# Q products of two token blocks by seven half-size products in place of eight, and two output products of a step moved into the next one

## The reference

```python
    Q = (q @ Wq.T).reshape(b, s, HKV, exp, DK)      # q = _layernorm(x), exp = 4, DK = 128
    K = (k @ Wk.T).reshape(b, s, HKV, DK)           # k = v = ctx
    V = (v @ Wv.T).reshape(b, s, HKV, DV)
    scores = jnp.einsum('bqhed,bkhd->bheqk', Q, K) * scale      # causal mask, softmax
    attn = jnp.einsum('bheqk,bkhd->bqhed', probs, V)
    return attn.reshape(b, s, H * DV) @ Wd.T
...
x = x + jnp.tanh(g_xattn[0]) * _L0_xattn_ref(_layernorm(x, axis=-1), ctx, ctx, Wq, Wk, Wv, Wd)
x = x + jnp.tanh(g_ffn[0]) * _L0_ffn_ref(_layernorm(x, axis=-1), qweight, scale, zero_point, bias)
```

## Time and profile before

| | before |
|---|---|
| median of 3 runs (lowest, highest) | 1063.35 us (1062.31, 1066.21) |
| the profiled execution, device time | 1062.54 us |
| its span, first to last instruction | 1060.6 us |
| PE busy | 1019.3 us, 96% |
| DVE busy | 685.5 us, 65% |
| ACT busy | 456.7 us, 43% |
| POOL busy | 235.5 us, 22% |
| mean granted TensorE clock | 0.994 |

### The profile page before, as it was taken

The page is one execution under the profiler, slowest core; times in us unless marked ns, Lnnn a source line. Parts: engine busy times, 40 slices in busy tenths (PEclk is TensorE's granted clock), DMA queues, the critical chain, the costliest instruction groups (busy, mean ns, idle before and its releaser), DMA issues.

```text
span 1060.6 us, 19976 instructions
## 1 busy us (share of the span) xinstructions
PE 1019.3 (96%) x7842; PEld 569.6 (54%) x7842; DVE 685.5 (65%) x1374; ACT 456.7 (43%) x917; POOL 235.5 (22%) x245
## 2 busy tenths in 40 slices
PE   4889999999998999999999999999999999999995
PEld 2455555555554555555555555555555555555542
DVE  5856677777578665765466556665556664555678
ACT  5777676676532343233334332244433323333322
POOL 1355565565604000210001200210000400000013
PEclk9999999999999999999999999999999999999998
DMA  7648655445355432444313643234333443223111
GB/s 276 217 155 286 209 163 186 160 132 158 103 176 200 96 87 96 159 130 136 107 56 112 198 138 122 78 121 120 126 117 118 131 136 115 62 96 134 69 37 60
DMA packets 90219, 142.61 MB, mean 134 GB/s; under 512 B 31248, under 2 KB 64016, under 8 KB 79504
## 3 DMA queue, kind: packets, MB, share of 16 engines
q1 hardware_dynamic: 90128, 141.34, 41.5%
...
## 4 chain that ended last, share of the span: by engine, by line
PE 86%; DVE 10%; ACT 2%; issue 2%; DMA 1%; SPq 0%; DVEq 0%; ACTq 0%
PE pa L1295 42%; PE py L1295 29%; PE av L1408 5%; PE pp L1391 3%; PE ps L1375 2%; PE py L1466 2%; PE pp L1375 2%; DVE q L897 1%; DVE wq L897 1%; DVE sc L943 1%; DVE row_max L941 1%; DVE sc L937 1%; DVE sc L954 1%; DVE xn L1053 1%; DMA xacc<-in_x 1%
## 5 line engine op out<-in xcount | busy, mean ns | idle before, releaser
L1295 PE MATMUL pa<-xT,wq 128*128 128x512 f16 x1536 | 344.4, 380 | 10.2 <-DVE q L897 7.5
L1295 PE MATMUL py<-wd,att 128*128 128x512 f16 x1488 | 336.2, 379 | 0.7 <-issue 0.7
L1295 PEld LDWEIGHTS pa<-xT,wq 128*128 128x128 f16 x1536 | 146.1, 98 | 192.0 <-issue 25.9
L1295 PEld LDWEIGHTS py<-wd,att 128*128 128x128 f16 x1488 | 143.2, 98 | 159.2 <-issue 1.1
L677 ACT ACTIVATE q<-pa 128x512 f16<-128x512 f32 x128 | 75.7, 591 | 264.8 <-PE pa L1295 264.8
L976 DVE SCALAR_TENSOR_TENSOR xacc<-py,f_y,xacc 128x512 f32<-128x512 f32 x128 | 95.7, 748 | 124.2 <-PE py L1295 124.2
L728 ACT ACTIVATE att<-av 128x256 f16<-128x256 f32 x256 | 80.8, 384 | 145.8 <-PE av L1408 145.3
L967 DVE SCALAR_TENSOR_TENSOR att<-av,att 128x256 f16<-128x256 f32 x256 | 93.5, 418 | 67.1 <-ACT att L728 66.9
L897 DVE SCALAR_TENSOR_TENSOR q<-pa,q 128x512 f16<-128x512 f32 x128 | 87.9, 686 | 58.7 <-ACT q L677 55.9
L1295 PE MATMUL pa<-wv,cT 128*128 128x128 f16 x1536 | 96.2, 219 | 0.0
L1295 PEld LDWEIGHTS pa<-wv,cT 128*128 128x128 f16 x1536 | 89.8, 98 | 0.9
...
## 6 DMA issues: line engine op xcount, KB each, us to landing
wq<-kept_q SPq DMA_DIRECT2D x24, 1024.0 KB, 7.1
wd<-kept_d SPq DMA_DIRECT2D x23, 1024.0 KB, 4.8
v_dup<-v_nat SPq DMA_DIRECT2D x128, 128.0 KB, 2.4
raw_d<-in_wdT SPq DMA_DIRECT2D x8, 1024.0 KB, 10.2
kept_q<-wq SPq DMA_DIRECT2D x8, 1024.0 KB, 8.0
kept_d<-wd SPq DMA_DIRECT2D x8, 1024.0 KB, 5.2
raw_q<-in_wqT SPq DMA_DIRECT2D x7, 1024.0 KB, 5.4
...
```

Source lines behind the costliest of these rows:

```text
L1295: last = pe.matmul(out, stationary(a, i), moving(b, i), start=(i == 0 and (a, b) == PASSES[0]), stop=(i == count - 1 and (a, b) == PASSES[ ...
```

## The change

Q of steps `m` = 16 to 31 (the last two blocks) is computed by the seven-product scheme: heads are taken in two pairs `r`, each weight pair and the activations are cut into quadrants (head x half of the contraction, half of the contraction x half of the tokens), and `run(m, r, i)` is one half product: 2 chunks x 3 passes = 6 matmuls of 256 columns. Seven runs for each pair, 14 for a step, replace four heads. Runs 5, 6, 7 and 4 take mixed operands (sums and differences of quadrants): mixed weights `ws` and mixed activations `tT`. ACT copies three partial results of a pair out of PSUM (`copy_p1`, `copy_p5`, `copy_u2`), DVE adds later ones to them (`add_11`, `add_22`, `add_12`), and ACT and DVE take HI and LO parts of four quadrants (`hi_*`, `lo_*`). `Q_SCALE` and the scaling of the squares change by a power of two.

The mixed weights are made in steps 13 to 20 (`mixing(n)` is the group): SP loads a group's raw weights again (`load_mix`), POOL mixes them (`mix_weights`), ACT and DVE split them (`mix_hi`, `mix_lo`), and SP keeps them (`keep_mix`) and brings them back in block 3 (`back_mix`). The mixed activations of blocks 2 and 3 are made in steps 12 and 20 (`mix_norm`, `mixed_hi`, `mixed_lo`) and transposed by 32 further DMA transposes each; 8 of the 32 plain ones fall away. The norm that feeds the next block is a step earlier in blocks 1 and 2 (step 3 of the block in place of 4), and `ffn_weight` is done in steps 9 and 10 in place of 8 and 9.

From step 14 on `y_unit(n, 2)` and `y_unit(n, 3)` are issued among the Q runs of step `n + 1`, with their `y_part`, and `back_d` behind the first transposes of a step. Tiles were moved to other storage to make room.

```diff
-            return 6 if tb == 0 else 4
+            return 6 if tb == 0 else 3
...
+        FIRST_FAST = 2 * GROUPS
+        RUN = ((0, 1), (0, 5), (0, 2), (0, 6), (0, 7), (0, 3), (1, 1), (1, 5), (1, 2), (1, 6), (1, 7), (1, 3))
+
+        def fast(m):
+
+            return FIRST_FAST <= m < STEPS
...
+        def deferred(n):
+
+            return fast(n + 2)
...
+        BANK_X, BANK_Y, BANK_Z = (pa[0], av[1]), (pa[1], pa[1]), (av[0], av[0])
...
+            def transpose_first(n):
+
+                g, tb = n % GROUPS, n // GROUPS
+                if tb > 0 and g in (1, 2):
+                    call = NORMS.index((2, tb - 1))
+                    transpose_norm(call, transposes(call)[16 * (g - 1):16 * (g - 1) + 8])
+                if 0 < tb < BLOCKS - 1:
+                    call = NORMS.index((1, tb + 1))
+                    if g in (4, 5):
+                        transpose_norm(call, transposes(call)[16 * (g - 4):16 * (g - 4) + 8])
+                    elif g == 6:
+                        transpose_mixed(tb + 1, MIXED[12:20])
+
+            def transpose_rest(n):
+
+                g, tb = n % GROUPS, n // GROUPS
+                if tb > 0 and g in (1, 2):
+                    call = NORMS.index((2, tb - 1))
+                    transpose_norm(call, transposes(call)[16 * (g - 1) + 8:16 * g])
+                if 0 < tb < BLOCKS - 1:
+                    call = NORMS.index((1, tb + 1))
+                    if g == 4:
+                        transpose_norm(call, transposes(call)[8:16])
+                    elif g == 5:
+                        transpose_mixed(tb + 1, MIXED[0:12])
+                    elif g == 6:
+                        transpose_mixed(tb + 1, MIXED[20:32])
...
+                if m + 1 >= FIRST_FAST + GROUPS and fast(m + 1):
+                    back_mix(m + 1)
+                transpose_first(n)
+                if fast(m) and n < LAST:
+                    back_d(n)
+                transpose_rest(n)
                 if m < STEPS:
                     duplicate_v(m)
                 if ffn_of(n) is not None:
                     for t in range(ffn_of(n) * TILES, (ffn_of(n) + 1) * TILES):
                         store(t)
+                if mixing(n) is not None:
+                    keep_mix(mixing(n))
+                if mixing(n + 1) is not None:
+                    load_mix(mixing(n + 1))
...
+                pool.tensor_tensor(a22, a22, a21, ALU.add).then_inc(s_mix, 1)
+                pool.tensor_tensor(a21, a11, a21, ALU.subtract).then_inc(s_mix, 1)
+                pool.wait_ge(s_mix, 4 * g + 2)
+                pool.tensor_tensor(a11, a22, a11, ALU.subtract).then_inc(s_mix, 1)
+                pool.wait_ge(s_mix, 4 * g + 3)
+                pool.tensor_tensor(a12, a12, a11, ALU.subtract).then_inc(s_mix, 1)
...
+                if mixing(n) is not None:
+                    mix_weights(mixing(n))
+                if mix_of(n) is not None:
+                    mix_norm(mix_of(n))
+                    for t in range(TILES):
+                        mixed_lo(mix_of(n), t)
...
+                if fast(m):
+                    copy_p1(m, 0)
+                    exp(n, 0)
+                    copy_p5(m, 0)
+                    copy_u2(m, 0)
+                    exp(n, 1)
+                    hi_11(m, 0)
+                    p_part(n, 0)
+                    p_part(n, 1)
+                    hi_22(m, 0)
+                    hi_12(m, 0)
+                    copy_p1(m, 1)
+                    hi_21(m, 0)
+                    copy_p5(m, 1)
+                    copy_u2(m, 1)
+                    hi_11(m, 1)
+                    hi_22(m, 1)
+                    hi_12(m, 1)
+                    p_transposed(n, 0)
+                    hi_21(m, 1)
+                    if mixing(n) is not None:
+                        mix_hi(mixing(n), (0, 1))
...
+            def add_22(m, r):
+
+                dve.wait_ge(r_mm, run_count(m, r, 7))
+                dve.wait_ge(p5_ok, pair_count(m, r))
+                dve.tensor_tensor(p5, half(BANK_X[r]), p5, ALU.add).then_inc(c22_ok, 1)
...
+                if fast(m):
+                    scores(n, 0)
+                    scores(n, 1)
+                    add_11(m, 0)
+                    normalise(n, 0)
+                    normalise(n, 1)
+                    p_part(n, 0)
+                    add_22(m, 0)
+                    add_12(m, 0)
+                    y_late(2)
+                    lo_11(m, 0)
+                    lo_22(m, 0)
+                    lo_12(m, 0)
+                    lo_21(m, 0)
+                    p_part(n, 1)
+                    add_11(m, 1)
+                    y_late(3)
+                    add_22(m, 1)
+                    add_12(m, 1)
+                    lo_11(m, 1)
+                    lo_22(m, 1)
+                    lo_12(m, 1)
+                    lo_21(m, 1)
+                    if ffn is not None:
+                        ffn_scaled(t0)
+                    k_part(m)
+                    if mixing(n) is not None:
+                        mix_lo(mixing(n), (0, 1))
...
+                if (r, i) == (0, 1):
+                    pe.wait_ge(q_back[m % 2], backs(m))
+                    if m < FIRST_FAST + GROUPS:
+                        pe.wait_ge(s_hi, HPG * (m - FIRST_FAST + 1))
+                        pe.wait_ge(s_lo, HPG * (m - FIRST_FAST + 1))
+                    else:
+                        pe.wait_ge(s_back[m % 2], 16 * ((m - FIRST_FAST - GROUPS) // 2 + 1))
+                    if m % GROUPS == 0:
+                        transposed(pe, NORMS.index((1, tb)))
+                        pe.wait_ge(t_ld, 16 * len(MIXED) * (tb - 1))
+                    pe.wait_ge(k_hi, m)
+                    pe.wait_ge(k_lo, m)
+                elif (r, i) == (0, 5):
+                    pe.wait_ge(v_hi, m)
+                    pe.wait_ge(v_lo, m)
+                elif (r, i) == (0, 2):
+                    pe.wait_ge(av_hi, 4 * (m - 1) - 1)
+                    pe.wait_ge(av_lo, 4 * (m - 1) - 1)
+                elif (r, i) == (1, 1):
+                    pe.wait_ge(av_hi, 4 * (m - 1))
+                    pe.wait_ge(av_lo, 4 * (m - 1))
+                elif (r, i) == (1, 5):
+                    pe.wait_ge(c12_ok, pair_count(m, 0))
+                elif (r, i) == (1, 2):
+                    pe.wait_ge(c11_ok, pair_count(m, 0))
+                elif i == 6:
+                    pe.wait_ge(p1_ok, pair_count(m, r))
+                elif i == 7:
+                    pe.wait_ge(u2_ok, pair_count(m, r))
+                elif i == 3:
+                    pe.wait_ge(p5_ok, pair_count(m, r))
+                elif i == 4:
+                    pe.wait_ge(c22_ok, pair_count(m, r))
...
+                for kc in range(2):
+                    for c, d in PASSES:
+                        first = kc == 0 and (c, d) == PASSES[0]
+                        last = pe.matmul(half(bank), a[:, c, head, w_half + kc, :], b[:, d, b_half + kc, at],
+                                         start=first and i in (1, 2, 5),
+                                         stop=kc == 1 and (c, d) == PASSES[-1],
+                                         skip_group_check=i in (3, 4, 6, 7))
...
+                    run(m, 0, 1)
+                    run(m, 0, 5)
+                    run(m, 0, 2)
+                    run(m, 0, 6)
+                    y_unit(n - 1, 2)
+                    run(m, 0, 7)
+                    run(m, 0, 3)
+                    run(m, 1, 1)
+                    run(m, 0, 4)
+                    run(m, 1, 5)
+                    run(m, 1, 2)
+                    run(m, 1, 6)
+                    y_unit(n - 1, 3)
+                    run(m, 1, 7)
+                    run(m, 1, 3)
+                    p_transpose(n, 0)
+                    run(m, 1, 4)
+                    if ffn is not None:
+                        ffn_unit(t0, n)
+                    k_unit(m)
...
+                if deferred(n):
+                    continue```

On PE the order of a step changes as follows. Before, in step 16 (`pp<-k,q` and `ps<-k,q` are the scores, `pa<-xT,wq` is Q, `pa<-cT,wk` is K, `pa<-wv,cT` is V):

```order
L1375 MATMUL pp<-k,q 128x32 x24
L1375 MATMUL ps<-k,q 128x64 x24
L1295 MATMUL pa<-xT,wq 128x512 x48
L1391 MATMUL pp<-ident,pr 128x128 x8
L1295 MATMUL pa<-cT,wk 128x512 x12
```

More of the change, by code:

```diff
@@ L26 @@
 STEPS = BLOCKS * GROUPS
+HB = BT // 2
+HK = D // 2
 HI, LO = 0, 1
@@ L801, in _ @@
                     v_part(m)
+                if mixing(n) is not None:
+                    mix_hi(mixing(n), range(HPG))
                 if prep:
@@ L1204, in _ @@
                 for j in range(TILES):
-                    if n < LAST - 1:
+                    if n < LAST - 1 and not (deferred(n) and j >= 2):
                         y_part(n, j)
```

412 lines of the change are left out of this document (327 added, 85 removed).

## The result

| | before | after |
|---|---|---|
| median (lowest, highest) | 1063.18 us (1062.31, 1066.21) | 1095.61 us (1094.52, 1098.63) |
| span of the profiled execution | 1060.6 us | 1092.9 us |

The ratio is 1.030, 95% interval 1.027 to 1.033: slower by 32 us. The direction was forecast (slower, 1076.0); the size lies outside the range, which ended at 1087.

The account below looks back on a forecast made before the run. PE, busy 96% of the span, was taken as the bound. From 1062.54 us: -23.0 - 4.6 + 0.4 + 1.3 + 19.7 + 14.6 + 5.1 = +13.5, giving 1076.0 us; range 1054 to 1087.

Parts of the forecast that it names:

- The columns: Q by fourteen runs: 84 matmuls at 0.109 us, 9.14 in place of 10.58; -1.44 us a step, -23.0 over 16.
- Block 1: Step 9's `ffn_weight` stall goes, -4.6; meeting `ln_bn` and `ln_stats`, +0.4; `mix_hi` ahead of `av_part` 2 in step 13, +1.3.
- `add_22` in a plain step: `run(m, 0, 4)` waits for DVE's addition, S - 0.9 with DVE starting its chain at S = +1.6: 0.7 us, bounds 0.5 to 0.9.
- DVE's extra work at a step's end makes S larger: S, DVE's chain start, comes later in steps with norm or `ffn_zero` tails; all `add_22` stalls together +19.7 us.
- rival (d): Worse: short waits cost clock too (+5), and POOL's mixing slows DVE or SP's lateness reaches K or V: 1088; chance 0.08.
- SP's queue: Late transposes and loads: PE waits 7.2 us in step 15, 3.6 in step 23, 3.8 for wd in step 20; +14.6.
- SP is also behind by some 2 us: Step 14: SP's lag from steps 12 and 13, raising the transposes' lateness for step 15 from 6.1 to 8.2 us.
- the wait of step 23: PE waits for block 3's mixed transposes, landing at +34.4 against PE's 30.8: +3.6 us, plus 1.65 for the clock.
- Step 20: 3.5 us on `add_22` from `ln_norm` and four `ffn_zero` (S = 4.4), 3.8 waiting for wd, 1.65 for the clock.
- ACT's copies fit between: Q runs: ACT copies partial results in time, p1 by +2.6 for a run at +3.3, so no wait was added.
- The clock: Waits longer than 2.9 us, in steps 15, 20 and 23, cost 1.65 us each, +5.1; shorter ones nothing.
- The rule that I weighed and set aside: The throttled clock is the default, so no wait is safe; pricing waits of steps 18, 19 and 26 would add 5 us.

Follow-up runs that it names:

- e9: The changed kernel, seven products only in steps 26 to 30, mixing in steps 12-15 and 21, block 2's norm back, last `ffn_zero` spread: 1052.78 us, 0.991 of before.
- e3: The changed kernel with no mixed weights or activations made, kept or transposed; runs read plain tiles, output not the reference's: 1060.03 us, 0.998 of the kernel before.
- e2: The changed kernel without POOL's mixing of weights; loads, splits and transposes stay, output not the reference's: 1090.10 us, 1.027 of the kernel before.
- e7: The changed kernel with `duplicate_v`, `keep_mix` and `load_mix` issued by POOL in place of SP: 1113.58 us, 1.048 of the kernel before.
- e8: The kernel with plain operands and none mixed, with the next block's norm again at step 4 of blocks 1 and 2: 1056.36 us, 0.994 of the kernel before.

## Why the prediction was right in direction and wrong in size

**The columns: right.** 0.109 us a matmul, 9.14 for Q: the plain step shows a run of 0.65 and lasts 29.11, within 0.04 of 28.83 + 0.24 of waiting. The gain of 1.44 us a step was there, 23 over 16 steps.

**Block 1: right**, -4.06 in step 9 against -4.6 + 0.4, and +1.35 in step 13 against +1.3. Step 12 lost 0.75 that had no term: PE waits there for a DVE split of Q, in the step in which the mixed activations are made; e9 shows the same 0.75 in step 20, to which it moves this, and in e3, which makes none, step 12 loses 0.3.

**`add_22` in a plain step: right in kind, 0.24 in place of 0.7 us.** Start to start the two additions and `p_part` take 0.33 or 0.34 each, not 0.41. That is 0.24 of the 0.32 by which the chain is shorter, 7.00 in place of 7.32; the 0.07 for an overlap at its end wasn't there either. The lower bound that I named, 0.34, was the right value for the addition, but the 0.5 us that I worked out from it was not.

**"DVE's extra work at a step's end makes S larger": right where POOL is quiet, mis-sized beside it.** The terms for steps 16 to 19 were 1.6, 0.85, 2.0 and 2.4, 6.85 together. After lost 14.0 there (3.0, 3.3, 2.8, 4.9 over 28.83, or 35.88 in step 19). Without POOL's mixing, e2, it is 7.4. Of the 6.6 us between the two, 1.7 are the clock in step 19. The failing step is that I took DVE's durations from step 22, a step in which POOL was quiet, and put POOL into rival (d), with 0.08, though step 9 of the same trace shows the slower ones. Rows of both engines in one step show it: 128x256 from two SBUF tiles took 1.48 us in place of 0.42. The Trainium skill, "GPSIMD Engine Reference", section "Specifications", says that GpSimd's SBUF interfaces are shared with VectorE, with contention for DVE instructions that have two SBUF inputs. The trace agrees, down to the addition with a PSUM input, which stays at 0.41.

**SP's queue: the mechanism right, the lag too small.** 26.7 us for 20 transposes held to 0.1. "SP is also behind by some 2 us" was the failing step: the transposes began at +9.45, where the sum had 4.7 and that lag of 2 on top. `duplicate_v` of the step before stood ahead (3.1 us), and the four loads of weights took 4.0 us from first issue to the first transpose, 499.76 - 495.78, in place of 2.15. The lag came from step 13, whose 20 transposes began only at +6.5. My own sum gave 8.2 us late, and I took 7.2 without a reason; that is 1 us of the miss. The wait was 11.1 us against 7.2 forecast, and step 15 13.8 over 28.83 against 8.9. e7 fits the lag: with the transposes at +2.3 the wait is 6.4.

In step 22 I gave 0.7, and it lost 5.6, and here too it is the lag that failed. By my numbers `back_d(22)` would be issued at 4.0 + 2.2 + 8 x 1.33 = +16.9 and land 4.8 later, ahead of PE, which wanted it at +23.1; I didn't write that down, but it gives no wait. It was issued at +21.2. I had step 21's mixed transposes begin at +14.4, when the y unit is done. But SP came late out of step 20: the eight plain transposes of step 21, which begins at 733.99, were issued from +6.5 to +18.6, and only then came `back_d(21)` and the twelve mixed ones:

```profile
740.47 12.14 SPq L467 DMA_TRANSPOSE xT<-xh  x8
752.71 0.53 SPq L430 DMA_DIRECT2D wd<-kept_d  x1
```

For the wait of step 23 I forecast 5.3 us with the clock, and 4.5 were measured: that fits the same lag, less what PE had already lost in step 22.

**Step 20: right in sum, 10.75 against 9.0, not in its parts.** PE waited 2.0 us for a copy by ACT, 2.3 for `add_22`, and 3.1 for `pT`; wd was in time. The first two are one cause. DVE began the step's scores at +6.3 (700.68 - 694.41), not at S = 4.4: three `ffn_zero` took 4.0 us, not 3 x 0.66, with POOL's `ln_lo` of the moved norm beside them. On ACT two of the copies stand behind `exp(n, 0)`, and that waited for DVE:

```profile
696.75 4.01 DVE L1438 SCALAR_TENSOR_TENSOR xacc<-ff_rows,small,xacc 128x512 f32<-128x512 f32 x3
...
703.49 1.49 DVE L1277 TENSOR_TENSOR sc<-sc,row_max 128x512 f32<-128x512 f32 x1
```

```profile
695.92 5.85 POOL L657 TENSOR_TENSOR xh<-xn,xh 128x512 f16<-128x512 f32 x4 [26.13 <-ACT xh L875]
```

```profile
702.10 0.42 ACT L887 ACTIVATE sc<-sc 128x256 f32<-128x256 f32 x1 [4.50 <-DVE sc L1277]
```

So "ACT's copies fit between" failed here, and DVE's term was mis-sized by POOL once more. The wait for `pT` goes in e2, with the mixing; there the wait for wd appears, which in the changed kernel was hidden behind it.

**The clock: the price right for a short wait, the condition wrong.** I priced waits of at least 2.9 us at 1.65 each and shorter ones at nothing. (Three waits at 1.65 are 4.95; my sum has 5.1.) Step 15 paid more: behind its 11.1 us PE worked 5.2 us, 527.93 to 533.12, with the clock granted at 0.50, which is some 2.6 us lost. After step 19's wait of 2.81 and step 26's of 2.06 the clock fell too, after step 18's of 2.55 it did not. The windows of 3.3 us behind these waits (busy, granted clock), in this order step 18, 19 and 26:

```profile
633.21:636.50 3.29, 3.29 (x28) 1.00 0.27 47
665.20:668.50 3.30, 3.30 (x21) 0.66 0.01 2
904.07:907.37 3.30, 3.30 (x21) 0.67 0.07 15
```

The rule that I weighed and set aside, that no wait is safe as such, would have added 5 us; two of its three waits, 3.3 us, came true.

**The sum.** Against the forecast the span lost 18.8 us more: steps 16 to 19 +7.2, step 15 +4.9, step 22 +4.9, step 20 +1.75, steps 21, 25 and 26 +3.6, steps 9 to 13 +0.95; steps 23, 24 and 27 to 30 gave back 2.8, and what lies ahead of step 8 1.6. Some 9 of it is SP's queue (steps 15, 22 and 23) and what the clock cost behind it, 7 POOL beside DVE (steps 16 to 19, clock included), the rest clock and small tails. Rival (d), at 1088, named POOL beside DVE and the clock behind short waits, and both came. It also named lateness on SP, but for K or V, where it was wd and the mixed activations that came late. I held these for mishaps, when POOL and SP were both busy in every one of the steps in which weights are mixed. That step 20 came out near its forecast is luck: its waits were others than the ones I had added up.

**What stays open.** Whether the transposes would be issued faster beside fewer other transfers was not tried. Which of DVE's tails makes the 7 us of step 20 that remain in e8 was not separated either, nor whether the products would pay in blocks 2 and 3 as a whole if `ffn_zero` and the norms were spread. The gain of e9 needs the steps that it leaves alone, so whether a sixth or seventh step would still pay there is not known.
